# Pairwise products of a recommendation tower: split products from a four-row stack, against fp32 products of 32-row weights with pauses between the gathers

## The reference, cut to what matters

```python
p = inputs[:, ROW, :]
q = inputs[:, COL, :]
z = jnp.einsum('bpc,apc,bpa->bp', p, w, q)      # 512 x 741
h = jnp.concatenate([z, dense_ctx], axis=1)     # 512 x 757
h = jnp.maximum(h @ W_top1 + b_top1, 0.0)       # 512
h = jnp.maximum(h @ W_top2 + b_top2, 0.0)       # 256
y = h @ W_top3                                  # 1
```

## Time and profile before

| what | value |
|---|---|
| times of the three runs | 220.49, 220.56, 225.24 us |
| span of the profiled execution | 285.0 us |
| the profiled execution's own time | not listed; only its span |
| TensorE busy, mean granted clock | 198.8 us, 0.844 |
| VectorE busy | 146.6 us |
| ScalarE busy | 97.5 us |
| GpSimd busy | 134.8 us |
| DMA | 31.40 MB in 11352 packets |

### The profile page before, as it was taken

How to read it: one execution, slowest core, us unless ns; L and a number is a source line. 1 busy time by engine, 2 the same in 40 slices (tenths; PEclk the granted TensorE clock), 3 DMA queues, 4 the chain that set the end, 5 groups by cost and what they waited for, 6 DMA issues and landing times.

```text
span 285.0 us, 2687 instructions
## 1 busy us (share of the span) xinstructions
PE 198.8 (70%) x974; PEld 73.5 (26%) x974; DVE 146.6 (51%) x115; ACT 97.5 (34%) x142; POOL 134.8 (47%) x134
## 2 busy tenths in 40 slices
PE   0048668453212277738798197699899999999996
PEld 0012223000000033213333032243333334344341
DVE  0353794101000027824794266389599779898230
ACT  2516899300000047830540071037127127110032
POOL 7774767777777300776587887200042015007000
PEclk9999797755555559795999669599999999999999
DMA  4869779700000003997266018148715846450000
GB/s 134 257 210 300 285 177 212 164 16 13 14 13 13 9 0 74 300 207 148 50 158 166 12 41 183 41 96 167 167 33 118 183 98 129 98 121 1 0 2 0
DMA packets 11352, 31.40 MB, mean 110 GB/s; under 512 B 3230, under 2 KB 7098, under 8 KB 10379
## 3 DMA queue, kind: packets, MB, share of 16 engines
q1 hardware_dynamic: 7882, 29.45, 42.1%
q0 software_dynamic: 3456, 1.78, 3.5%
HBM read 12.34 MB, written 0.00 MB: 43 GB/s over the span
## 4 chain that ended last, share of the span: by engine, by line
PE 51%; issue 18%; DMA 9%; DVE 7%; SPq 6%; another core or an unknown queue 4%; ACT 3%; DVEq 0%; ACTq 0%
PE t_ps L719 16%; PE z_ps L735 15%; PE z_ps L688 9%; DMA mlp<-tbl 6%; PE side_ps L750 5%; DMA wring<-w_lo 4%; DVE prod L658 3%; SPq L425 2%; PE t_ps L777 2%; DVE prod L629 2%; SPq L431 1%; SPq L475 1%; PE t_ps L765 1%; PE t_ps L770 1%
## 5 line engine op out<-in xcount | busy, mean ns | idle before, releaser
L658 DVE TENSOR_TENSOR prod<-t_ps,eT 128x1536 f32<-128x1536 f32 (+2 forms) x70 | 109.9, 1600 | 79.3 <-PE t_ps L719 49.7
L514 POOL DMA_INDIRECT gathered<-tbl,ids_sb x108 | 104.9, 971 | 53.5 <-issue 31.4
L719 PE MATMUL t_ps<-stack,wring 128*128 128x512 f32 x210 | 72.9, 464 | 12.2 <-issue 6.7
L735 PE MATMUL z_ps<-prod,sel 128*32 128x512 f32 x380 | 57.5, 645 | 4.6 <-issue 4.6
L719 PEld LDWEIGHTS t_ps<-stack,wring 128*128 128x128 f32 x210 | 38.3, 205 | 65.8 <-issue 39.5
L688 PE MATMUL z_ps<-prod,room 125*32 125x512 bf16 x72 | 21.0, 534 | 34.1 <-issue 33.3
L528 POOL TENSOR_TENSOR room<-room,w_hi 128x512 f32<-128x512 f32 x3 | 3.9, 1286 | 66.3 <-ACT w_hi L603 66.3
L629 DVE TENSOR_SCALAR prod<-mlp,slice_rows 125x2048 bf16<-125x2048 f16 x18 | 14.8, 856 | 23.0 <-remote 23.0
L587 ACT ACTIVATE stack<-hi_lo 32x512 fp32r<-32x512 f32 x39 | 24.6, 629 | 2.6 <-issue 1.2
L580 ACT ACTIVATE stack<-eT 32x512 fp32r<-32x512 f32 x39 | 24.4, 625 | 1.0 <-PE t_ps L719 0.7
L750 PE MATMUL side_ps<-room,mlp 128*128 128x512 f32 x32 | 18.4, 660 | 7.7 <-ACT eT L567 7.6
(11 more groups left out here) (49 smaller groups left out, 113.5 us busy)
## 6 DMA issues: line engine op xcount, KB each, us to landing
wring<-w_hi SPq DMA_DIRECT2D x30, 224.0 KB
wring<-w_lo SPq DMA_DIRECT2D x30, 224.0 KB
stack<-stack SPq DMA_DIRECT2D x9, 512.0 KB
w_lo<-wst SPq DMA_DIRECT2D x4, 896.0 KB, 15.2
eT<-hot_ids SPq DMA_DIRECT2D x3, 1024.0 KB
gathered<-tbl,ids_sb POOLq DMA_INDIRECT x108
mlp<-w SPq DMA_DIRECT2D x1, 1536.0 KB
mlp<-tbl SPq DMA_DIRECT2D x12, 125.0 KB
```

Source lines behind the costliest of these rows:

```text
L514: pool.indirect_dma_start(gathered[:, n % GATHER_BUFS, b, K * r:K * r + K], None, tables[f], bass.IndirectOffsetOnAxis(ap=ids_sb[:, F * b ...
L658: dve.tensor_tensor(prod[:, g % XSLOTS, 0:n, :], t_ps[g % 2][:, 0:n, :], field, ALU.mult).then_inc(multiplied, 1)
L719: mm = pe.matmul(t_ps[g % 2][:, i, :], wring[:, c % WSLOTS, passes % WCHUNK, :].bitcast(F32R), stack[:, J % STACKS, src - G * J, :].bitcas ...
L735: mm = pe.matmul(z_ps[K * (u % G):K * (u % G) + K, :], sel[:, u // G, :], prod[:, g % XSLOTS, t - TILE_BASE[g], :], start=(u < G), stop=(u ...
```

## The change: what it does

- **Products.** `stack`, `hi_lo`, `w_hi`, `w_lo` and `wring` go, with the steps that fill them. All weights stay in one array `w_sb` (55 tiles of 128 x 128 fp32). A tile is now an fp32 product of 32 rows of weights with 32 rows of `eT`; the four fields of a block lie on four row ranges, and each writes a PSUM bank of its own. A diagonal block is two products of 64 rows. The tiles are 190 as before. Work goes by "quads" (J, I) of up to four tiles, in pairs: VectorE multiplies two tiles (128 x 1024) at a time; three pairs of PSUM banks, six buffers of `prod`.
- **Lookups.** Four blocks of fields are looked up (0, 1, 2, 4), with 34 slices. Tables are laid out by block and not split by arithmetic: the upper half of each fp32 word is read as bf16 in place (every second element), and ScalarE turns the two lower bytes to bf16 (two instructions for each block). The two halves of the result are written back by two copies, as bf16 and as 16-bit integers. The indices come as 16 x 512 and are spread over the partitions by products with a 0/1 matrix.
- **Gathers.** Six blocks (3, 5 to 9), 23 fields, 92 indirect DMAs, a buffer for each block. After each field but the last GpSimd clears a 128 x 1280 fp32 array twice, each clear waiting for the one before.
- **Dense layer.** Rounds of blocks of z are [0, 1], [2, 3], [4] in place of one block each; "long" and "late" steps go; the last block of z starts its own accumulation. Its weights are loaded at the start, after the pair weights.

The core of the diff, in the order of the file:

```diff
-HOT_BLOCKS = [0, 1, 3]
+LOOKED = [0, 1, 2, 4]
+PAIRS = [(q, i, min(2, QUADS[q][2] - i)) for q in range(NQUAD) for i in range(0, QUADS[q][2], 2)]
+TSLOTS = 3
+XSLOTS = 6
-ROUNDS = [[0], [1], [2], [3]]
+ROUNDS = [[0, 1], [2, 3], [4]]
+KEEP_LEAD = 3
+PAUSE = 1280
+PAUSES = 2
...
+    for q in range(4, NQUAD):
+        J = QUADS[q][0]
+        steps.append(("quad", q))
+        since += 1
+        for T in GATHERED[1:]:
+            if q == FIRST_QUAD[T] - KEEP_LEAD:
+                steps.append(("keep", T))
...
+            for J, r in fields:
+                f = BLOCKS[J][r]
+                for b in range(NCHUNK):
+                    pool.indirect_dma_start(
+                        gathered[J][:, b, K * r:K * r + K], None, tables[f],
+                        bass.IndirectOffsetOnAxis(ap=ids_sb[:, F * b + f:F * b + f + 1], axis=0),
+                    ).then_inc(rows_in[J], 16)
+                for _ in range(PAUSES if (J, r) != fields[-1] else 0):
+                    if pauses:
+                        pool.wait_ge(paused, pauses)
+                    pool.memset(pause[:, :], 0.0).then_inc(paused, 1)
+                    pauses += 1
...
+                elif step[0] == "lower":
+                    h = step[1]
+                    act.wait_ge(tab_in[h], 16 * len(tab_pieces))
+                    for i in range(2):
+                        act.activation(lower[i][h][0:HP, :, :], bytes_of[h][0:HP, :, 1 - i::4], ACT.Copy,
+                                       scale=256.0 if i == 0 else 1.0).then_inc(lower_made, 1)
...
+                        s = 2 * (p % TSLOTS)
+                        dve.tensor_tensor(prod[:, p % XSLOTS, 0:n, :], ps[:, s:s + n, :],
+                                          eT[:, I:I + 1, :].broadcast_to([P, n, B]), ALU.mult).then_inc(multiplied, 1)
...
+                    for p in range(NPAIR):
+                        if PAIRS[p][0] != q:
+                            continue
+                        _, first, n = PAIRS[p]
+                        if p >= TSLOTS:
+                            pe.wait_ge(multiplied, p - TSLOTS + 1)
+                        for i in range(first, first + n):
+                            rows = source_rows(q, i)
+                            mm = pe.matmul(ps[:, 2 * (p % TSLOTS) + i - first, :], w_sb[rows, w_tile(q), :],
+                                           eT[rows, J, :], start=True, stop=True)
+                        mm.then_inc(t_made, 1)
```

More of the change, by code:

```diff
@@ L73 @@
[L73 to L76, removed]
+HP = 125
+LOOKED = [0, 1, 2, 4]
+GATHERED = [J for J in range(NBLK) if J not in LOOKED]
+NHOT = len(LOOKED)
+SMALL = [f for f in range(F) if TABLE_ROWS[f] == 1000] + [f for f in range(F) if TABLE_ROWS[f] == 1250]
+HOT_FIELDS = [SMALL[G * h:G * h + G] for h in range(NHOT)]
+NSLICE = [TABLE_ROWS[fields[0]] // HP for fields in HOT_FIELDS]
+assert all(TABLE_ROWS[f] == HP * n for fields, n in zip(HOT_FIELDS, NSLICE) for f in fields)
+SLICE_BASE = [sum(NSLICE[:h]) for h in range(NHOT)]
@@ new lines @@
+ROW_SETS = sorted(set(NSLICE))
+HOT_BUFS = 6
+_rest = [f for f in range(F) if not any(f in fields for fields in HOT_FIELDS)]
+BLOCKS = []
+for _J in range(NBLK):
+    if _J in LOOKED:
+        BLOCKS.append(HOT_FIELDS[LOOKED.index(_J)])
+    else:
+        BLOCKS.append(_rest[:G])
+        _rest = _rest[G:]
+assert not _rest
+FIELDS_IN = [len(fields) for fields in BLOCKS]
+DIAGONAL = [[(0, 1), (0, 2), (1, 3)], [(2, 1), (3, 0), (3, 2)]]
+LAST_DIAGONAL = [(2, 0), (0, 1), (1, 2)]
+QUADS = []
+for _J in range(NBLK):
+    QUADS += [(_J, _I, FIELDS_IN[_J]) for _I in range(_J)]
+    QUADS.append((_J, _J, 2 if FIELDS_IN[_J] == G else 1))
@@ L77 @@
+FIRST_TILE = [TILE_BASE[q] + i for q, i, _ in PAIRS]
+PAIRS_THROUGH = [sum(1 for p in PAIRS if p[0] <= q) for q in range(NQUAD)]
+TSLOTS = 3
+XSLOTS = 6
 ZTILES = P // G
 ZM = ZTILES // G
[L81 to L109, removed]
@@ L126, with sources @@
-FIRST_GROUP = [min(g for g in range(NGROUP) if GROUPS[g][0] == J) for J in range(NBLK)]
-ROUNDS = [[0], [1], [2], [3]]
[L128 to L133, removed]
-SEL_LAG = 2
+NZ = -(-NTILE // ZTILES)
+ROUNDS = [[0, 1], [2, 3], [4]]
+SEL_LAG = 2
+KEEP_LEAD = 3
+PACE = 2
+Z_LAG = 2
+PAUSE = 1280
+PAUSES = 2
+def sources(q):
+    J, I, n = QUADS[q]
+    if I < J:
+        return [[(r, c) for c in range(G)] for r in range(n)]
+    if FIELDS_IN[J] == G:
+        return DIAGONAL
+    return [LAST_DIAGONAL]
@@ L137, in plan @@
+_free = [z_row(t, c) for t in range(NTILE) for c in range(G) if (t, c) not in _taken]
+DENSE_ROWS = []
+while len(DENSE_ROWS) < NDENSE // 2:
+    _a, _b = _free[:2]
+    if _a // P == _b // P:
+        DENSE_ROWS.append((min(_a, _b), abs(_a - _b)))
+    _free = _free[2 if _a // P == _b // P else 1:]
+DENSE_BLOCKS = sorted({first // P for first, _ in DENSE_ROWS})
 def plan():
     steps, done = [], 0
-    early = [(m, n, i) for n in range(len(ROUNDS)) for m in range(M1) for i in range(len(ROUNDS[n]))]
@@ L156, in plan @@
[L156 to L161, removed]
+    early = [(m, n) for n in range(len(ROUNDS)) for m in range(M1)]
+    since = 0
     def sums(upto, exact):
@@ L184, in plan @@
[L184 to L204, removed]
@@ L205, in plan, with there @@
-    sums(NGROUP - 2, True)
-    steps += [("early", *e) for e in early]
[L207 to L212, removed]
+    def there(zb):
+        names = [s[:2] for s in steps]
+        return ("z", zb) in names and sum(s[0] == "quad" for s in names[names.index(("z", zb)):]) > Z_LAG
@@ new lines, in plan @@
+    steps += [("ids", 0), ("lower", 0), ("ids", 1), ("look", 0, 0, 3), ("lower", 1), ("ids", 2), ("look", 0, 3, 8),
+              ("keep", 0), ("lower", 2), ("ids", 3), ("look", 1, 0, 8), ("lower", 3), ("keep", 1), ("look", 2, 0, 8),
+              ("keep", 2), ("quad", 0), ("look", 3, 0, 2), ("quad", 1), ("look", 3, 2, 5), ("quad", 2),
+              ("look", 3, 5, 8), ("quad", 3), ("look", 3, 8, 10), ("keep", 4), ("keep", 3)]
+    sums(1, True)
+    for q in range(4, NQUAD):
[5 more added lines that the diff above has]
+                steps.append(("keep", T))
+        near = any(0 < FIRST_QUAD[T] - KEEP_LEAD - q <= 1 for T in GATHERED)
+        if early and since >= PACE and not near and all(there(zb) for zb in ROUNDS[early[0][1]]):
+            steps.append(("early", *early.pop(0)))
+            since = 0
+        sums(q - SEL_LAG, False)
+        sums(q - SEL_LAG - 1, True)
@@ L215 @@
+    sums(NQUAD - 2, True)
+    steps += [("early", *e) for e in early]
+    sums(NQUAD - 1, True)
+    return steps
 PLAN = plan()
-LAST_FIRST = [M1 - 1] + list(range(M1 - 1))
-assert NGROUP % 2 == 0
-SPLITS = [s[1:] for s in PLAN if s[0] == "split"]
 TURNS = [s[1] for s in PLAN if s[0] == "keep"]
-assert all([s[1] for s in PLAN if s[0] == part] == TURNS for part in ("halve", "stack"))
+SUMS = [s for s in PLAN if s[0] == "sums"]
+EARLY = [s[1:] for s in PLAN if s[0] == "early"]
+SUMS_THROUGH = [next(i + 1 for i, s in enumerate(SUMS) if s[1] + s[2] >= FIRST_TILE[p] + PAIRS[p][2])
+                for p in range(NPAIR)]
@@ L223, in turns @@
+assert sorted(TURNS) == list(range(NBLK))
+assert [T for T in TURNS if T in LOOKED] == LOOKED and [T for T in TURNS if T in GATHERED] == GATHERED
 def turns(J):
     return TURNS.index(J) + 1
[L228 to L245, removed]
 def lay_out_weights(w, W_top1):
-    wst = np.zeros((NWCOL, G, K, WCHUNK, G, K), w.dtype)
+    wst = np.zeros((G, K, WTILES, G, K), w.dtype)
     w1 = np.zeros((NZ * P, H1), W_top1.dtype)
[L256 to L268, removed]
+    for q, (J, I, n) in enumerate(QUADS):
+        for i, tile in enumerate(sources(q)):
+            for src, c in tile:
+                a, b = BLOCKS[J][src], BLOCKS[I][c]
+                block = w[:, pair_of(a, b), :]
+                wst[src, :, w_tile(q), c, :] = block if a > b else block.T
+                w1[z_row(TILE_BASE[q] + i, c)] = W_top1[pair_of(a, b)]
@@ L347, in dlrm_tower @@
+        tab_in = [sem(f"tab_in{h}") for h in range(NHOT)]
+        w_in = [sem(f"w_in{J}") for J in range(NBLK)]
         mlp_in = sem("mlp_in")
@@ new lines, in _ @@
+            sp.dma_start(hot_ids_sb[:, :], hot_ids).then_inc(hot_ids_in, 16)
+            load_table(0)
+            load_table(1)
+            load_table(2)
+            for J in range(3):
+                load_w(J)
+            load_table(3)
+            for J in range(3, NBLK):
+                load_w(J)
+            for dst, src in mlp_loads:
+                sp.dma_start(dst, src).then_inc(mlp_in, 16)
+            for step in PLAN:
+                if step[0] == "z" and step[1] in DENSE_BLOCKS:
@@ L590, in _ @@
                 elif step[0] == "z":
                     act.wait_ge(summed, step[2])
[L592 to L595 removed]
+                    act.activation(z_sb[:, step[1], :], z_ps, ACT.Copy).then_inc(z_kept, 1)
+                elif step[0] == "early":
+                    m, n = step[1:]
+                    i = EARLY.index((m, n))
+                    act.wait_ge(early_made, i + 1)
@@ L767, in _ @@
```

(10 more changed lines are left out.)

569 lines of the change are left out of this document (202 added, 367 removed).

## The result

| | before | after |
|---|---|---|
| median of the timed runs | 221.72 us (220.49 to 225.24, 4 runs) | 233.71 us (232.90 to 234.53, 4 runs) |
| ratio | | 1.0522, 95% interval 1.0476 to 1.0568 |
| the profiled execution: time, span, mean granted clock | span 285.0 us, 0.844 | 232.91 us, 231.2 us, 0.926 |
| busy: TensorE, VectorE, ScalarE, GpSimd | 198.8, 146.6, 97.5, 134.8 us | 198.5, 145.3, 41.7, 154.8 us |
| DMA | 31.40 MB | 9.74 MB |

What follows compares the result with a forecast made beforehand. TensorE bound the kernel before; afterwards GpSimd's late rows decide. Head 57, stages with waits to 211, restart 2.5 to 213.5, end 15.4: span 229, plus 3.8 makes 233 us; forecast 226 to 240, range 214 to 250.

Steps and rivals of the forecast that it cites:

- GpSimd's chain: Gathers and clears: a field takes 7.4 us, so rows of block 7 arrive at 121, block 8 at 150, block 9 at 173.
- rival 1: Gathers: GpSimd isn't late in timed runs, since its gathers or their gaps are shorter; 213 us, 3.5% faster, chance 0.17.
- The products: 32-row fp32 products on TensorE: four lie nearly side by side, 1.06 us, between bounds of 0.99 and 3.44.
- rivals 2 and 3: Products: pairs hardly overlap, 249 us or near 262, chance 0.17; or no overlap at all, 300 us, chance 0.07.
- The wait and its price: TensorE at transposes: waits for block 7 from 111 to 121, block 8 from 143 to 150; then 2.5 us at half clock.
- The stages behind block 8: Quads 34 to 42 take 26 us, to 176; quads 43 to 54 take 34.7, to 211; 213.5 with the restart.
- The head: Lookups before the general stage: ScalarE's queue holds block 2 until about 38; 3 us for slowed comparisons; general stage starts at 57.
- Before's own time: Profile of the kernel before: holes of 68 us aren't in timed runs, leaving a span of 217 against the timed 220.56.
- the remainder around a span: Time outside the profiled span in a timed run: 3.8 us, added to the forecast span of 229.
- Rival 4: Clears between gathers: holes were partly in timed runs, and the pauses give back at most 3.8 us, 229; no separate chance.

Runs made afterwards that it cites:

- e3: Changed kernel with four clears after each field in place of two, chip A: 290.08 us, 1.295 of the kernel before.
- e6: e5 with the two clears for each field kept, chip A: 232.62 us, 1.047 of the kernel before.
- e8: Kernel before with two clears added after each gathered field but the last, chip A: 275.68 us, 1.239 of the kernel before.
- e1: Changed kernel without the clears between fields, chip A: 220.55 us, 0.984 of the kernel before.
- e5: Changed kernel without clears, the fourth lookup's comparisons put ahead of the preceding quad in VectorE's list, chip A: 203.11 us, 0.912 of before.
- e4: Changed kernel with all off-diagonal products reading the same 32 rows, output wrong, chip A: 421.5 us, 1.881 of the kernel before.
- e9: e5 with fields 2 and 3 of a block reading the rows of fields 0 and 1, output wrong, chip B: 342.85 us, 1.183 of before.
- e7: Kernel before, unchanged, run and profiled again on chip A: 221.5 us.
- e12: e5 with one clear for each field, on chip C: 209.19 us, 0.943 of the kernel before.
- e10: e5 with one clear for each field, on chip B: 222.63 us, 0.755 of the kernel before.
- e2: Changed kernel with one clear for each field in place of two, chip A: 223.81 us, 1.004 of the kernel before.

## Why the prediction was right, and where it was not

**GpSimd's chain (right).** A field takes 7.26 us (115.92 to 123.18), 7.4 forecast; a clear 1.20 on average, 1.17 forecast from two small ones. Block 7's transposes start at 122.06 and block 8's at 151.00, against 121 and 150; block 9's rows come in time (transposes at 175.00). e3, e6 and e8 show that the chain decides, e1 and e5 what is left without it: rival 1 gave 213 for a GpSimd that isn't late, and e1, in which it isn't, took 215.5 at best and 220.6 in the median.

**The products (right).** 1.06 to 1.14 us a quad; e4 and e9 measured what rivals 2 and 3 would have looked like, 1.99 (1.85 forecast) and 3.69 (3.44).

**The wait and its price (right in kind, the sizes off).** TensorE was to wait 10 us for block 7 and 7 for block 8; it waited 2.62 and 3.33, since it came 7 us later out of the head and the stage between the two blocks took 25.6 us, for 22.5. It made no difference, because the arrivals were right and a wait ends with the arrival. Only block 8 was to restart at half clock for 2.5 us; the four groups above took 1.86 and 1.52 for 0.99 and 1.07, which is 1.3 us of it. By the length of the stage the restart cost 1.6 us (24.0 from block 8's transposes to block 9's, for 22.4 in e5); block 7's stretch has a clock of 0.91 as well.

**The stages behind block 8 (two sizes off, nearly cancelling).** From block 8's transposes to block 9's the sum had 26 us and 2.5 for the restart; it was 24.0. From there to the last sums it had 34.7 us; it was 40.9, in this kernel (175.00 to 215.91) as in e5 (146.20 to 187.12). So the last sums ended at 215.9, 213.5 forecast. From there to the end it was 15.3 us, 15.4 forecast.

**The head (wrong, without effect).** The general stage was to start at 57 and started at 64. The step that failed took ScalarE's queue as what holds the fourth lookup, and quads and slices as if they followed each other freely. The runs showed VectorE's order instead (e5: 47 us), and the clears' effect on comparisons: 955 ns for one where e1 has 754, so 34 x 0.2 = 6.8 us, where I added 3 out of a possible 14. It cost next to nothing, because TensorE had to wait for blocks 7 and 8 anyway; e6 shows that. The Trainium skill (GPSIMD Engine Reference, Key points) has this contention as one of shared SBUF interfaces, with some kinds of VectorE's instructions. Here the trace agrees for memsets: the comparisons slow down and the multiplications don't, with a mean of 1165 ns in both kernels. That the comparison is of the kind the page names isn't shown.

**Before's own time (two errors that cancel).** Taking the holes for something that profiling does, and timed runs don't have, is the step that failed: on chip B they are there in timed runs as well, and cost about 70 us. My corrected span of 217 was 219.8 in e7, and the remainder around a span 1.7 us, not 3.8. The same remainder stands in the forecast: 229 + 3.8 = 233 against a measured 231.2 + 1.7 = 232.9. The span was 2 us too short and the remainder 2 us too long, so that the number came out within 1 us is in part luck; the forecast was good to some 2 us. Rival 4 was wrong as well: I priced what the pauses give back at 3.8 us at most. The kernel with one pause is some 15 us faster than before on chip C (e12) and 70 us on chip B (e10), so some 55 us of that are the holes.

What stays open: the changed kernel itself and e5 were not run on chip B. By e9 I would expect e5 to be slow there and by e10 the change to be fast, but that is argued. e9 alone doesn't separate this from its own longer products. Every run with long holes but the first profile comes from one session on chip B, so whether they belong to the chip or to something else of that session isn't separated; "chip B" stands for both here. Why a run of gathers starves the other engines there and not elsewhere isn't settled either; the traces have no semaphore and no queue that would name it.

## What to carry to other kernels

Put the arrival time of each block's rows beside the place in the list where TensorE takes them: a delay on the issuing engine is free until the two meet and then costs all of it (at most +3 us for the first clear, +10 to +12 for the second, +54 to +56 for two more). When a profile is much longer than the timed runs, time the same kernel on other chips before calling it an effect of profiling, and judge a safeguard by what it saves in the bad place as well as by what it costs in the good one: one clear costs 6 us where e5 takes 203, and where gathers starve the rest the kernel with it takes 223 us and before 292. When two engines alternate within a stage, let each one's list produce what the other needs next before it waits for the other. That swap gave 17 us by the medians, 11 by the profiled spans, and everything else of the change, without its clears, 3.

## What the runs showed of the hardware, unexpected

- A run of indirect gathers, 1.25 us each, held up nearly every other engine in the session on chip B (13 matmuls in 30 us, e9) and none on chip A (e1, e7); the same kernel took 292 and 222 us.
- The granted clock was 0.57 on average, so mostly the lower of the two levels (1.2 and 2.4 GHz), over 100 us in which TensorE was busy 99.56 us with products of the same 32 rows (e4); with two ranges (e9) and four (e5) it stayed at 1.00.
- One kernel (e1) with idle stretches of 2 to 3 us in its head varied by 8.5 us between runs, with mean granted clocks of 0.938 to 0.976; without them (e5) it was 2.5 us, at 1.00 in all runs.
- Clears on GpSimd stretched VectorE's 16-bit comparisons, from 754 ns each without them (e1) to 927 with one for each field (e2), 955 with two and 1190 with four (e3), and left its multiplications at 1165 ns in all four.
